# A loop of data-dependent feeding steps: the next step read from token 0 through a lookup table, its weights requested earlier, and the attention bodies of two engines written as engine loops

## What is computed

```python
NB, NOPS, D, H = 33, 19, 32, 128
def step(h, p):
    op = argmax(h[0, 0, :NOPS])
    q, k, v = h @ p['wq'][op], h @ p['wk'][op], h @ p['wv'][op]
    y = softmax(q @ k.T * scale) @ v @ p['wo'][op]     # per batch of 256 tokens
    h = where(p['am'][op], y, h)
    z = relu(h @ p['w1'][op] + p['b1'][op]) @ p['w2'][op] + p['b2'][op]
    h = where(p['fm'][op], z, h)
    return h
out, _ = scan(step, x, params)       # 33 steps
t = t + out                          # the residual
```

## Time and profile before

| | us |
|---|---|
| median of 3 runs | 602.98 |
| lowest and highest run | 601.33, 608.59 |
| span of the profiled execution | 606.4 |
| busy in it: DVE, PE, POOL, ACT | 481.7, 419.3, 340.5, 196.1 |

### The profile page before, as it was taken

The page is one execution under the profiler, slowest core; times in us unless marked ns, Lnnn a source line. Parts: engine busy times, 40 slices in busy tenths (PEclk is TensorE's granted clock), DMA queues, the critical chain, the costliest instruction groups (busy, mean ns, idle before and its releaser), DMA issues.

```text
span 606.4 us, 8743 instructions
## 1 busy us (share of the span) xinstructions
PE 419.3 (69%) x3283; PEld 206.2 (34%) x3283; DVE 481.7 (79%) x605; ACT 196.1 (32%) x221; POOL 340.5 (56%) x303
## 2 busy tenths in 40 slices
PE   6787854656677667666776898999283997454851
PEld 2452323222232223222222344577252436331320
DVE  1999998899999999999999336989936569984242
ACT  2665793323323322323322062410021045112210
POOL 6767103659999998999999431699960000520000
PEclk8977987769999999999999989955575995567567
DMA  8640023935554556445451000000000000000000
GB/s 286 182 141 9 3 79 80 211 94 142 148 155 146 149 147 165 140 139 175 143 152 51 0 13 2 1 2 2 2 24 0 1 0 2 1 2 9 3 5 35
DMA packets 29523, 46.11 MB, mean 76 GB/s; under 512 B 18146, under 2 KB 19588, under 8 KB 28452
## 3 DMA queue, kind: packets, MB, share of 16 engines
q1 hardware_dynamic: 27044, 45.12, 26.2%
q0 software_dynamic: 2368, 0.37, 0.5%
q10 hardware_dynamic: 64, 0.00, 0.0%
HBM read 43.57 MB, written 1.11 MB: 74 GB/s over the span
## 4 chain that ended last, share of the span: by engine, by line
DVE 33%; POOL 29%; PE 19%; issue 13%; ACT 3%; DMA 2%; DVEq 1%; ACTq 0%; POOLq 0%; SPq 0%
POOL dBu L888 14%; POOL hit L872 6%; PE ps L2035 4%; POOL work L965 3%; DVE hC L1546 3%; PE ps L2363 2%; DVE hC L1316 2%; POOL work L970 2%; DVE hst L1525 2%; POOL work L954 2%; DVE hC L1312 2%; PE ps L2542 2%; PE ps L2532 1%; DVE work L1798 1%; PE ps L2243 1%
## 5 line engine op out<-in xcount | busy, mean ns | idle before, releaser
L2173 PE MATMUL ps<-hC,ident 128*128 128x512 f32 x256 | 122.4, 600 | 0.0
L1163 ACT ACTIVATE ps<-work,a_neg 128x1020 f32<-128x1020 f32 x64 | 71.2, 1115 | 153.9 <-DVE hst L1525 102.7
L1525 DVE TENSOR_TENSOR_SCAN hst<-ps,dBu 128x1024 f32<-128x1024 f32 x43 | 98.3, 2286 | 5.1 <-POOL dBu L888 3.8
L2157 PE MATMUL ps<-late,pick_state 96*128 96x512 bf16 x128 | 40.4, 398 | 70.4 <-DVE hC L1546 68.3
L872 POOL DMA_INDIRECT hit<-in_L_attn_edge_values,tab_i x64 | 64.8, 1012 | 29.5 <-DMA hit<-in_L_attn_edge_values,tab_i 20.1
L888 POOL TENSOR_TENSOR dBu<-work,dA 128x1024 f32<-128x1024 f32 x32 | 75.4, 2360 | 6.7 <-DMA dA<-b_rows_all 4.0
L2173 PEld LDWEIGHTS ps<-hC,ident 128*128 128x128 f32 x256 | 49.6, 194 | 43.3 <-issue 34.9
L888 POOL TENSOR_TENSOR dBu<-work,b_sb 128x1024 f32<-128x1024 f32 x16 | 39.6, 2475 | 38.7 <-DVE dA L1454 37.2
L1546 DVE TENSOR_TENSOR hC<-hst,ps 128x1024 f32<-128x1024 f32 x43 | 51.5, 1197 | 1.8 <-PE ps L2157 1.0
L1525 DVE TENSOR_TENSOR_SCAN work<-ps,dBu 128x1024 f32<-128x1024 f32 x21 | 48.0, 2286 | 2.6 <-POOL dBu L888 1.8
L2157 PEld LDWEIGHTS ps<-late,pick_state 96*128 96x128 bf16 x128 | 7.9, 98 | 121.8 <-DVE hC L1546 116.4
(11 more groups left out here) (374 smaller groups left out, 821.9 us busy)
## 6 DMA issues: line engine op xcount, KB each, us to landing
dA<-b_rows_all SPq DMA_DIRECT2D x64, 256.0 KB
b_sb<-b_rows_all SPq DMA_DIRECT2D x32, 256.0 KB
work<-b_rows_all SPq DMA_DIRECT2D x32, 256.0 KB
work<-in_L_attn_edge_index SPq DMA_DIRECT2D x6, 1024.0 KB, 6.5
dA<-in_L_attn_edge_index SPq DMA_DIRECT2D x1, 1024.0 KB, 5.0
dBu<-in_L_attn_edge_index SPq DMA_DIRECT2D x1, 1024.0 KB, 8.3
hit<-in_L_attn_edge_values,tab_i POOLq DMA_INDIRECT x64
late<-work SPq DMA_DIRECT2D x12, 64.0 KB, 2.0
```

Source lines behind the costliest of these rows:

```text
L1163: nc.scalar.activation(dst[:, :, 1:], src[:, :, 1:], ACT.Exp, scale=a_neg[:, n:n + 1]).then_inc(dA_sb, 1)
L1525: V.tensor_tensor_scan(h_buf[i % 3], dA_ps[k], dBu[:, k, :], 0.0, ALU.mult, ALU.add).then_inc(scan_done, 1)
L2157: last = T.matmul(bank(2 + h), pick_state[:, n, :, :].rearrange("p v i -> p (v i)"), parts[:, j * NT + h * HALF:j * NT + (h + 1) * HALF], ...
L2173: last = T.matmul(bank(6 + h), ident[:, :], hC[:, i % 2, h * HALF:(h + 1) * HALF], start=False, stop=(n == S - 1))
```

## The change

- The table. `step_table` (DVE, before `norm(4)`) replaces `step_codes`, `top_codes` and `drop_blocks`: a row of 19 x 34 integers, built by a running maximum, that gives for an operation and the number of blocks left the code of the next step. Its constants are filled by POOL after the Mamba scan. `find_step` ends with the index of the maximum; each engine reads that index and then the table's entry (`load_step`: two register loads).
- Token 0 first. PE computes token 0's hidden column (`first_hid`, with b1 as a row), ACT applies relu, PE computes its 32 outputs as a row in bank 7 (`first_out`, with b2), and DVE takes maximum and index from there. The widening of groups 0 to 3 stands around these: `widen(0)`, `first_out`, `widen(1)`, `widen(2)`, a wait for `ctrl_ready`, `widen(3)`, since bank 7 is shared.
- Weights. SP requests w1, b1 as a row, a first copy of w2 and b2 as a row as soon as the index is known and the widening done, and the copies b1_4, w2_4 and b2_4 as they come free.
- Work split. ACT takes groups 0 to 2 of the relu, DVE group 3. Both halves of `h4` (ACT) and of `x_out` (DVE) come straight from PSUM; `x_out` before the loop is formed by POOL. SP leaves the loop by itself and waits for the last sum (`summed`).
- 6 `keep_warm` matmuls before the step instead of 4, none behind it.
- The attention bodies of ACT and DVE are engine loops over the 16 batches; that of PE stays unrolled. PE's wait for `attn_dve` moves into the attention body.

The core of the diff:

```diff
+        def load_step(eng, active, op, done):
+
+            eng.reg_load(op, best8_i[0:1, 0:1])
+            best = eng.snap(op, min_val=0, max_val=NOPS - 1)
+            after = NB if done is None else (done >> 2) - 1
+            at = (best * ROWS + after).with_bounds(min_val=0, max_val=TABLE - 1)
+            eng.reg_load(active, next_step[0:1, bass.ds(at, 1)])
...
-        FFN_PE = G + 2
-        FFN_ACT = 3
-        FIND, AFTER = 5, 4
-        LINKS = 2 + FIND + AFTER
-        FFN_DVE = 2
+        FFN_PE = G + 1
+        FFN_ACT = 5
+        FFN_DVE = 1
+        PE_FREE, ACT_FREE, SUMS = 2, 3, 2
...
-                at = (STEPS - (code >> 2)).with_bounds(min_val=0, max_val=STEPS - 1)
+                best = sp.snap(op, min_val=0, max_val=NOPS - 1)
+                at = sp.snap((best + NOPS * NB - (code >> 2) * NOPS).with_bounds(min_val=0, max_val=STEPS - 1))
+                with sp.If(feeds > 0):
+                    hold(sp, ffn_pe, FFN_PE * i + 1)
+                    dst, src = step_weight(w1_4, "ffn_w1", at)
+                    sp.dma_start(dst, src).then_inc(dma_f, 16)
+                    sp.dma_start(b1_row, step_row("ffn_b1", at)).then_inc(dma_f, 16)
+                    dst, src = step_weight(w2_first, "ffn_w2", at, 1)
+                    sp.dma_start(dst, src).then_inc(dma_g, 16)
+                    sp.dma_start(b2_row, step_row("ffn_b2", at)).then_inc(dma_g, 16)
+                with sp.Else():
+                    sp.sem_inc(dma_f, 32)
+                    sp.sem_inc(dma_g, 32)
...
                     with sp.If(feeds > 0):
-                        dst, src = step_weight(w1_4, "ffn_w1", at)
-                        sp.dma_start(dst, src).then_inc(dma_f, 16)
                         hold(sp, ffn_act, FFN_ACT * i + 1)
+                        hold(sp, ffn_dve, FFN_DVE * i + 1)
                         sp.dma_start(b1_4, step_vector("ffn_b1", at, 1)).then_inc(dma_b1, 16)
+                        hold(sp, ffn_pe, FFN_PE * i + 2)
                         dst, src = step_weight(w2_4, "ffn_w2", at, 1)
-                        sp.dma_start(dst, src).then_inc(dma_g, 16)
-                        sp.dma_start(b2_4, step_vector("ffn_b2", at, G)).then_inc(dma_g, 16)
+                        sp.dma_start(dst, src).then_inc(dma_w2b, 16)
+                        hold(sp, ffn_act, FFN_ACT * i + 3)
+                        hold(sp, summed, SUMS * i + 1)
+                        sp.dma_start(b2_4, step_vector("ffn_b2", at, G)).then_inc(dma_b2, 16)
...
+                sp.reg_mov(taken, SUMS * i + (SUMS + 1))
                 hold(sp, ctrl_ready, i + 2)
-                sp.reg_load(active, ctrl[0:1, 0:1])
-            sp.wait_ge(x_new, 2 * 6)
+                load_step(sp, active, op, code)
+            sp.wait_ge(filled, FILLED["sum"])
+            hold(sp, summed, sp.snap(taken, min_val=1, max_val=SUMS * ALL_LEVELS + 1))
...
+            pool.wait_ge(x_new, 2 * 5)
+            pool.wait_ge(normed, 2 * 4 + 1)
+            nc.gpsimd.tensor_tensor(x_out, X[:, :], h4, ALU.add).then_inc(filled, 1)
...
+                    hold(act, first_pe, 2 * i + 1)
+                    nc.scalar.activation(hid_first, first_hid, ACT.Relu).then_inc(first_act, 1)
                     hold(act, dma_b1, 16 * i + 16)
-                    for g in range(2):
-                        hold(act, ffn_pe, FFN_PE * i + g + 1)
+                    for g in range(3):
+                        hold(act, ffn_pe, FFN_PE * i + PE_FREE + g + 1)
                         nc.scalar.activation(hid[:, g * NT:(g + 1) * NT], bank(2 * g, 2), ACT.Relu,
                                              bias=b1_4).then_inc(ffn_act, 1)
-                    hold(act, ffn_pe, FFN_PE * i + G + 2)
-                    hold(act, step_chain, LINKS * i + 1)
-                    hold(act, dma_g, 32 * i + 32)
-                    nc.scalar.activation(h4, bank(0, 2), ACT.Identity, bias=b2_4).then_inc(ffn_act, 1)
+                    hold(act, dma_b2, 16 * i + 16)
+                    hold(act, ffn_pe, FFN_PE * i + PE_FREE + FFN_PE)
+                    act.wait_ge(filled, FILLED["sum"])
+                    for h in range(2):
+                        if h == 1:
+                            hold(act, summed, SUMS * i + 2)
+                        nc.scalar.activation(h4[:, half(h)], bank(h), ACT.Identity, bias=b2_4).then_inc(ffn_act, 1)
                 with act.Else():
+                    act.sem_inc(first_act, 1)
...
+            def step_table():
+
+                dve.wait_ge(dma_m, 32)
+                dve.wait_ge(filled, FILLED["mask"])
+                by_block = table_in.rearrange("p (o r) -> p r o", r=ROWS)
+                blocks = lambda t: t.rearrange("p (b o) -> p b o", o=NOPS)
+                V.memset(by_block[:, 0:1, :], 0.0)
+                link(V.scalar_tensor_tensor(step_kinds, steps_u8[:, STEPS:], 2.0, steps_u8[:, 0:STEPS],
+                                            ALU.mult, ALU.add))
+                link(V.scalar_tensor_tensor(by_block[:, NB:0:-1, :], blocks(step_kinds), 0.0, blocks(code_base),
+                                            ALU.is_gt, ALU.mult))
+                link(V.tensor_tensor(by_block[:, NB:0:-1, :], by_block[:, NB:0:-1, :], blocks(step_kinds), ALU.add))
+                link(V.tensor_tensor_scan(table_out, table_keep, table_in, 0.0, ALU.mult, ALU.max))
+                link(V.tensor_copy(next_step, table_out))
+
+            step_table()
...
-            def find_step(link):
-
-                link(V.max(best8[:, :], h_t[0:1, 0:NOPS]))
-                link(V.max_index(best8_i[:, :], best8[:, :], h_t[0:1, 0:NOPS]))
-                link(V.tensor_tensor(one_hot[:, :], ops_at[:, :], best8_i[:, 0:1].to_broadcast([1, NOPS]),
-                                     ALU.is_equal))
-                link(V.tensor_tensor(one_hot[:, :], top_codes, one_hot[:, :], ALU.mult))
-                link(V.max(code8[:, :], one_hot[:, :]))
-                return V.tensor_copy(ctrl[:, :], code8[:, 0:1])
-
-            def drop_blocks(link):
-
-                link(V.tensor_scalar(later[:, :], code_top[:, :], code8[:, 0:1], None, ALU.is_lt))
-                link(V.tensor_tensor(codes_left, codes, later[:, :].unsqueeze(2).to_broadcast([1, NB, NOPS]),
-                                     ALU.mult))
-                link(V.tensor_reduce(top_codes, codes_left.rearrange("p b o -> p o b"), AX_X, ALU.max))
+            def find_step(scores, link):
+
+                link(V.max(best8[:, :], scores[0:1, 0:NOPS]))
+                return V.max_index(best8_i[:, :], best8[:, :], scores[0:1, 0:NOPS])
...
+                    with dve.Fori(0, B) as b:
+                        done = [0]
+                        alink = counted(attn_chain, ATTN_LINKS * i + 3 * b, done)
+                        hold(dve, attn_pe, ATTN_PE * i + ATTN_V + 1 + 3 * b)
...
+                    hold(dve, first_pe, 2 * i + 2)
+                    slink(V.max(best8[:, :], first_out[:, 0:NOPS]))
+                    V.max_index(best8_i[:, :], best8[:, :], first_out[:, 0:NOPS]).then_inc(ctrl_ready, 1)
+                    dve.sem_inc(step_chain, 1)
                     hold(dve, dma_b1, 16 * i + 16)
-                    for g in range(2, G):
-                        hold(dve, ffn_pe, FFN_PE * i + g + 1)
-                        V.tensor_scalar(hid[:, g * NT:(g + 1) * NT], bank(2 * g, 2), b1_4, 0.0, ALU.add,
-                                        ALU.max).then_inc(ffn_dve, 1)
-                    hold(dve, ffn_pe, FFN_PE * i + G + 1)
-                    hold(dve, dma_g, 32 * i + 32)
-                    V.tensor_scalar(h_col, bank(0)[0:C, 0:C], b2_4[0:C, :], None,
-                                    ALU.add).then_inc(step_chain, 1)
-                    hold(dve, step_chain, LINKS * i + 1)
-                    V.transpose(h_t, h_col).then_inc(step_chain, 1)
+                    hold(dve, ffn_pe, FFN_PE * i + PE_FREE + G)
+                    V.tensor_scalar(hid[:, 3 * NT:4 * NT], bank(6, 2), b1_4, 0.0, ALU.add,
+                                    ALU.max).then_inc(ffn_dve, 1)
+                    hold(dve, dma_b2, 16 * i + 16)
+                    hold(dve, ffn_pe, FFN_PE * i + PE_FREE + FFN_PE)
+                    dve.wait_ge(filled, FILLED["sum"])
+                    for h in (1, 0):
+                        if h == 0:
+                            hold(dve, ffn_act, FFN_ACT * i + ACT_FREE + 4)
+                        V.scalar_tensor_tensor(x_out[:, half(h)], bank(h), b2_4, X[:, half(h)], ALU.add,
+                                               ALU.add).then_inc(summed, 1)
                 with dve.Else():
                     dve.sem_inc(ffn_dve, FFN_DVE)
-                    dve.sem_inc(step_chain, 1)
-                    V.transpose(h_t, h4[0:C, 0:C]).then_inc(step_chain, 1)
-                hold(dve, step_chain, LINKS * i + 2)
-                done = [2]
-                slink = counted(step_chain, LINKS * i, done)
-                find_step(slink).then_inc(ctrl_ready, 1)
```

(51 more changed lines are left out.)

## The result

| | before | after |
|---|---|---|
| median of the runs, us | 602.15 (600.88 to 608.59, 4 runs) | 596.9 (595.85 to 597.8, 4 runs) |
| ratio, 95% interval | | 0.9871 (0.9832 to 0.991) |
| span of the profiled execution, us | 606.4 | 596.1 |

The change is faster by 1.3%, less than 2%. Applied to the 602.98 us that the prediction started from, the ratio makes 595.2: inside the range, a gain of 7.8 us where the prediction has 12.1.

The account below looks back on a forecast made before the run. It took PE's wait for VectorE's queue (5.5 us) and VectorE's loop exit before the output as binding: 606.4 - 5.1 - 0.8 - 6.2 = 594.3, carried to the median as 590.9 us, range 586.8 to 599.5.

Parts of the forecast that it names:

- turn of the loop: Between the steps: PE turns its loop, warms and starts the next step 2.6 us after narrowing.
- last narrowing to sum: End of each step: the halves of h4 and of the sum, with hops, finish 1.75 us after narrowing.
- Before the loop: Up to the first real matmul: -0.5, +0.85 load, +0.9 warming, -1.2 wait for VectorE; 564.6 us, no change.
- the rival of a fetch in every turn: PE's bigger loop body costs a code fetch a turn, +10.1 us, +3.4 for the clock: 607.8, median 604.4; chance 0.06.
- The step at either clock: First real matmul to end of narrowing: 9.1 us at full clock, 14.1 at half.
- The clock: TensorE's granted clock rises from 0.50 to 1.00 halfway through `widen(0)`, since PE has nearly no pause; narrowing ends 574.5.
- Kept: 9.1 us; dropped and regained in `widen(0)`: 10.8: Second step's length, depending on whether the pause before it drops the clock; 9.95 us was taken.
- the clock rises late: Rival: the clock rises only under the later groups; first narrowing ends near 576.9, gain 7.2 us, median 595.8; chance 0.23.
- The base: Savings were subtracted from one 606.4 us execution; its 3.4 us above the median 602.98 was carried over, giving 590.9.
- The serial widening: In each step, `widen(0)` alone holds the array 1.7 us at clock 1.00, 3.4 at 0.50, nearly what all four take.
- The end: After the last sum, VectorE's loop exit ends the kernel 5.5 us later, at 594.3; gain 6.2 us.
- The hidden pieces: `step_table` takes 4.8 us in VectorE's idle 5.35 us before 450.61; removing `step_codes` gives nothing; POOL's work is hidden.

Follow-up runs that it names:

- a_again: The changed kernel run once more with no edit; ratio to the kernel before 0.9888, span 598.3 us.
- a_unroll: The changed kernel with the attention bodies of ScalarE and VectorE unrolled as before; ratio to the kernel before 0.9899.
- b_again: The kernel before run once more with no edit, for a second profile; ratio 1.0017, span 601.5 us.
- a_nowarm: The changed kernel without its six warming matmuls; ratio to the kernel before 0.992.
- a_late_out: The changed kernel with SP's output waiting again for VectorE behind its loop; ratio to the kernel before 0.9933.
- a_order: The changed kernel with `first_out` ahead of `widen(0)`; ratio to the kernel before 0.9785, median 590.8 us.
- a_order_split: The changed kernel with `first_out` ahead of `widen(0)` and the relu split two groups each on ScalarE and VectorE; ratio to the kernel before 0.9807.
- a_order_nowarm: The changed kernel with `first_out` ahead of `widen(0)` and without its six warming matmuls; ratio to the kernel before 0.9839.
- b_tail: The kernel before with SP leaving the loop by itself and waiting for a semaphore VectorE raises with each sum; ratio to the kernel before 0.9934.
- b_wait: The kernel before with PE's wait for `attn_dve` moved into the attention body; ratio to the kernel before 0.9931.
- b_both: The kernel before with PE's wait for `attn_dve` moved and SP leaving the loop by itself; ratio to the kernel before 0.9893, median 597.52 us.
- a_two: The changed kernel with `widen(0)` and `widen(1)` both ahead of `first_out`; ratio to the kernel before 0.9896.

## Why the prediction was right in direction and too large

| us in the profile | forecast | after |
|---|---|---|
| first real matmul | 564.6 | 563.8 |
| step 1 (to its last narrowing) | 9.9 | 11.85 |
| turn of the loop | 2.6 | 2.06 |
| step 2 | 9.95 | 11.5 |
| last narrowing to sum | 1.75 | 1.7 |
| sum to end | 5.5 | 5.2 |
| end | 594.3 | 596.1 |

*Before the loop: right.* The first real matmul is at 563.8 (561.6 to 565.7 in the versions of the change that warm, 562.5 to 564.5 in those of before that keep the wait). That spread lies ahead of the last norm: behind it, it is 7.7 us in after, a_again and a_unroll and 7.6 in before and b_again. The wait for VectorE paid for the added load and warming. Nor is the 0.8 us between forecast and after in the table's first line a gain of the loop: the norm itself came 0.8 us sooner (556.10, in before 556.91). PE's branch over its body took 4.26 us the first time and 0.22 the second, like the earlier trace rows; the rival of a fetch in every turn would need a second long branch, and there is none:

```profile
L2529 PEldq COMPARE_BRANCH  x2: 217/2238/4260, 556.3 to 575.6; - x2
```

*The step at either clock: right.* I had 9.1 us at 1.00 and 14.1 at 0.50; a_again shows 9.0 and 14.8, a_nowarm 13.9 (its last microsecond at 1.00) and 14.3.

*The clock: the step that failed.* "I take it halfway through `widen(0)`" and "Kept: 9.1 us; dropped and regained in `widen(0)`: 10.8" priced both steps at 19.85 us. The four profiles with this order and warming have 23.3 to 23.8. The mistake was the shape: I let the clock rise once and stay, because PE has no pause, and it fell again with PE busy all through. (I had also read its rise in before a little late: it came at 573.9 and 591.0, 0.5 and 0.8 us before the narrowing ended, not with the warming behind it.) Of the rivals, "the clock rises late" had the number (595.8, by the ratio 595.2) but the mechanism only in part: in after and a_late_out the clock was early and didn't hold, in a_again and a_unroll it rose late, after the whole of step 1, and then held. That term is 3.5 us; an earlier start (0.8), a shorter turn (0.5) and a shorter end (0.3, with roundings) gave 1.7 back, which makes the 1.8 us between 594.3 and 596.1. Why two so different courses of the clock end within 0.5 us of each other isn't shown; that the term is 3.5 us in the usual execution rests on these four profiles.

*The base: a second error.* I subtracted from one execution and carried the difference over to the median. That execution was the slowest of the four runs of before and had narrowing nearly wholly at 0.50 in both steps; b_again has 39.0 us from the first real matmul to the end where it had 41.9. So, by this one other profile, 2.9 of the 12.1 us were that execution's. 12.1 less 2.9 less 1.8 is 7.4, and the ratios of after and a_again give 7.8 and 6.8. The sign that was at hand: the span stood 3.4 us above the median, and I carried it over as if it lay ahead of the loop.

*The serial widening.* At full clock it is nearly free: 9.0 us a step (a_again and a_unroll, step 2) against 9.1 and 8.7 in a_order. At half clock it costs 2.5 to 3: 14.8 against the 11.7 of a_order_split's first step, which had 1.00 for its last 0.6 us. Whether the order also makes the clock hold is less sure: both steps fell in after and a_late_out and neither in a_order, but step 2 held in a_again and a_unroll and fell in a_order_nowarm. The Trainium skill (TensorE: Matmul & The Clock Gate, Why this matters for your kernels) asks for 32-row matmuls in distinct row groups to run together; the runs bear it out, by those half-clock steps and by a_order, which comes nearest to it and is 5.2 us faster.

*The end: right.* VectorE's exit ends the kernel 5.2 us after the sum, and b_tail and a_late_out price the output's wait behind it: 2.9 and 3.2 us by the traces, 4.0 and 3.7 by the ratios, where 3.5 and 3.6 were expected.

*The hidden pieces: right, but for one margin.* The table's lines on VectorE:

```profile
445.83 0.78 DVE L1785 SCALAR_TENSOR_TENSOR late<-late 1x627 f32<-1x627 uint8 x1
...
446.64 1.32 DVE L1787 SCALAR_TENSOR_TENSOR late<-late 1x627 f32<-1x627 f32 x1
448.00 1.32 DVE L1789 TENSOR_TENSOR late<-late 1x627 f32<-1x627 f32 x1
449.35 1.49 DVE L1790 TENSOR_TENSOR_SCAN late<-late 1x646 f32<-1x646 f32 x1
...
451.40 0.69 DVE L1435 TENSOR_TENSOR xn<-ps,rstd 128x512 f32<-128x512 f32 x1
```

It took 5.5 us against the forecast's 4.8 (whose terms make 4.5): two operations (L1787, L1789) write the table transposed and backwards, the innermost step being 34 floats, and cost 1.32 each, not 0.80. The norm behind it no longer waits at all in after; its second half still waits 0.47 us for ScalarE. The cover is used up to the last tenth there; in a_again the norm still waits 0.36 us. The step's weights came ahead of need, as said: w1 was requested at 571.64 and needed at 577.7, 6.1 us later, and where PE did wait for it, it could start 3.6 us (b_wait) and 3.0 us (b_both) after the request.

**What stays open.** Why the clock holds in a_order and falls in after. "A single group in the array" is excluded both as what is needed for a fall (a_two fell with two groups together, a_order_nowarm with four) and as enough for one (a_again held under one). The clock's changes also fall differently in two executions of one program, which no edit here controls. That a_order wins is shown by the times. That it wins through the clock is shown by its profile and agreed with by the mean clocks of its six executions, but a_order_split, with the same order on PE, had one step at each clock, and a part of the gain is that the new order loses less at half clock; the two parts aren't separated.

## What to carry to other kernels

Before summing savings against a profiled execution, look at where it differs from the median, and take stages whose duration depends on the granted clock at both levels: here that was worth 2.9 of 12.1 us. When a small early result must be had out of a large matmul stage, put its few tiny matmuls ahead of the whole stage and take the short wait (0.44 us), rather than splitting one group off to cover it. And look for the two lines behind a large change first: one moved wait and an output that no longer waits for VectorE's exit gave a ratio of 0.9893 by themselves, the whole change 0.9871. The rest of the change, the table and token 0 first, began to pay only with `first_out` ahead of the widening (0.9785).

## What the runs showed of the hardware

- The granted clock fell from 1.00 to 0.50 while TensorE ran matmuls without a pause (567.9 and 581.6 in after). With such a fall inside it the widening took 1.5 times as long (4.4 us for the 12 matmuls that took 2.88 at 1.00 in a_again).
- Matmuls of several row groups cost hardly more than those of one: at 0.50 one group's four instructions take 3.76 us (a_again), two groups' eight 3.78 (a_two), four groups' sixteen 3.82 (before); at 1.00 one takes 1.96 and two 1.99. Where the fourth group's calls wait for the index, the sixteen take 2.88 at 1.00 (a_order) and 4.67 at 0.50 (a_order_split).
- One program's two steps had clocks of 0.50 and 1.00 in one execution (a_again), and a mix in both in another (after), at nearly the same total (23.8 and 23.4 us).
- From its last operation in a nest of four engine loops to its first behind it, VectorE takes 4.94 us in a_late_out and 5.08 in b_again, with branches and register loads alone.
- VectorE's one-partition operations on 627 elements take 0.78 to 0.80 us in order and 1.32 when they write with a step of 34 floats (L1787, L1789).
